# A ring of sixteen pairs of one-hot tiles in the routing stage of a layer with sixteen thousand routed rows, and another place for four products of each expert

## What is computed

```python
logits = xf @ gate_w.T
rw, sel = jax.lax.top_k(logits, TOP_K)          # TOP_K = 2
rw = jax.nn.softmax(rw.astype(jnp.float32), axis=-1).astype(x.dtype)
for e in range(E):                              # E = 8
    we = jnp.sum(jnp.where(sel == e, rw, 0.0), axis=-1)
    h = jax.nn.silu(xf @ w1[e].T) * (xf @ w3[e].T)
    out = out + h @ w2[e].T * we[:, None]
```

## Time and profile before

| what | us |
|---|---|
| median of 3 runs | 3086.04 |
| lowest and highest of them | 3084.84, 3086.20 |
| the execution that the profile shows | 3087.87 |
| its span, first to last instruction | 3086.1 |
| the routing stage in it, L1566 to L1664 | 2248.7 to 2339.6 |

### The profile page before, as it was taken

The page is one execution under the profiler, slowest core; times in us unless marked ns, Lnnn a source line. Parts: engine busy times, 40 slices in busy tenths (PEclk is TensorE's granted clock), DMA queues, the critical chain, the costliest instruction groups (busy, mean ns, idle before and its releaser), DMA issues. The chain is left out here.

```text
span 3086.1 us, 63036 instructions
## 1 busy us (share of the span) xinstructions
PE 2895.5 (94%) x22889; PEld 1807.5 (59%) x22890; DVE 2292.1 (74%) x4040; ACT 1939.0 (63%) x3559; POOL 683.5 (22%) x957
## 2 busy tenths in 40 slices
PE   5899999985999999999999999998888999999998
PEld 4777777773333333333333333337767888888886
DVE  5777777765999999999999999957775444444543
ACT  3666666660788888888888888875533333333332
POOL 2222222221000000000000000001102555555554
PEclk8998999986999999999999999998889999999999
DMA  1222332223122222222222222216642333333332
GB/s 45 97 97 96 110 110 97 101 92 104 50 82 71 85 68 66 65 71 71 72 68 69 66 67 71 72 41 211 215 138 47 50 51 48 50 49 51 49 49 41
DMA packets 170809, 243.18 MB, mean 79 GB/s; under 512 B 30952, under 2 KB 118272, under 8 KB 170576
## 3 DMA queue, kind: packets, MB, share of 16 engines
q1 hardware_dynamic: 121984, 170.70, 18.0%
q0 software_dynamic: 31152, 52.33, 8.7%
q10 hardware_dynamic: 17440, 16.98, 1.7%
HBM read 126.53 MB, written 111.21 MB: 77 GB/s over the span
## 5 line engine op out<-in xcount | busy, mean ns | idle before, releaser
L1002 DVE TENSOR_REDUCE b_mxq<-b_p_m 128x1 f32<-128x1024 f32 x1024 | 1222.1, 1222 | 70.8 <-PE b_p_m L1025 63.6
L926 ACT ACTIVATE b_probs<-b_p_e 128x512 f32<-128x512 f32 x2048 | 1105.6, 597 | 146.4 <-PE b_p_e L1073 37.8
L1025 PE MATMUL b_p_m<-b_kst,b_qst 64*128 64x512 f32 x2048 | 765.2, 454 | 26.1 <-DMA b_vst<-v_d 21.9
L1073 PE MATMUL b_p_e<-b_qst,b_kst 64*128 64x512 f32 x2048 | 747.4, 444 | 0.2 <-ACT b_probs L926 0.2
L1044 PE MATMUL b_p_o<-b_probs,b_vst 128*32 128x256 f32 x8208 | 642.1, 390 | 0.5 <-ACT b_probs L926 0.4
L1073 PEld LDWEIGHTS b_p_e<-b_qst,b_kst 64*128 64x128 f32 x2048 | 315.8, 184 | 419.3 <-ACT b_probs L926 354.9
L1812 ACT ACTIVATE d_act<-d_p_up 128x512 f32<-128x512 f32 x136 | 81.3, 598 | 491.4 <-PE d_p_up L1885 491.4
L1044 PEld LDWEIGHTS b_p_o<-b_probs,b_vst 128*32 128x32 f32 x8208 | 168.2, 108 | 324.2 <-issue 186.8
L1025 PEld LDWEIGHTS b_p_m<-b_kst,b_qst 64*128 64x128 f32 x2048 | 319.9, 188 | 57.2 <-DVE b_mxq L1002 30.9
L1781 POOL DMA_INDIRECT out_dram<-d_y,d_to x136 | 217.8, 1601 | 216.5 <-DVE d_y L1846 203.9
L1900 PE MATMUL d_p_y<-w2T,d_hT 128*128 x1096 | 259.1, 379 | 0.8 <-ACT d_hT L1806 0.8
(11 more groups left out here) (312 smaller groups left out, 4131.6 us busy)
## 6 DMA issues: line engine op xcount, KB each, us to landing
b_qst<-qk_d SPq DMA_DIRECT2D x384, 64.0 KB
b_kst<-qk_d SPq DMA_DIRECT2D x384, 64.0 KB
qk_d<-a_hi SPq DMA_DIRECT2D x32, 512.0 KB, 2.8
qk_d<-a_lo SPq DMA_DIRECT2D x32, 512.0 KB, 3.7
v_d<-a_v_s SPq DMA_DIRECT2D x16, 1024.0 KB, 4.5
b_vst<-v_d SPq DMA_DIRECT2D x64, 256.0 KB
o_d<-b_oT POOLq DMA_DIRECT2D x63, 256.0 KB, 2.7
raw<-in_L_ffn_w_dram SPq DMA_DIRECT2D x24, 512.0 KB, 4.9
```

Source lines behind the costliest of these rows:

```text
L926: nc.scalar.activation(probs[(2 * step + e % 4 // 2) % BUFS][:, (e % 2) * 512:(e % 2 + 1) * 512], p_e[(slot(e) if more1 else e) % EB][:], ...
L1002: V_.reduce_max(mxq[half][:, h, qt:qt + 1], p_m[j % 2][:], AX.X).then_inc(s["m_red"], 1)
L1025: mm(p_m[j % 2][:, kh * 512:(kh + 1) * 512], qst[r][rows(h), qt * P:(qt + 1) * P], kst[r][rows(h), kh * 512:(kh + 1) * 512], start=True, s ...
L1073: mm(p_e[u % EB][:], kst[r][rows(h), kt * P:(kt + 1) * P], qst[r][rows(h), a * 512:(a + 1) * 512], start=True, stop=True).then_inc(s["e_ps ...
```

## The change

- RING goes from 4 to 16. The pairs lie in two large tiles, `lo_tiles` and `hi_tiles`. To make room, some tiles that only the preparation uses (`iota_i`, `val_i`, `slot_i`, `of_i`, `hi_i`, `lo_i`, `first`) now share their space with ring places 8 to 15. Their instructions stay as they are.
- The four `rest` products of an expert stand between its eighth and its ninth column, no longer ahead of the first.
- `own`, `end_of` and `past` come right behind `other` on VectorE, ahead of the first pair. `p_ex` is multiplied right behind `p_rank`, in expert 0. One semaphore, `rank_ps`, is gone: `ranks` waits on `ex_ps`. `experts_of_tiles` follows `ranks`, ahead of expert 1's pairs.

```diff
+    RING = 16
+    lo_tiles, hi_tiles = sb("lo_tiles", [P, RING, P]), sb("hi_tiles", [P, RING, WIDE])
+    is_lo, is_hi = [lo_tiles[:, r] for r in range(RING)], [hi_tiles[:, r, 0:TILES] for r in range(RING)]
+    spare = [hi_tiles[:, r].bitcast(i32) for r in range(8, 14)]
...
-    RING = 4
-    is_lo = [sb(f"is_lo{r}", [P, P]) for r in range(RING)]
-    is_hi = [sb(f"is_hi{r}", [P, TILES]) for r in range(RING)]
...
         V_.tensor_scalar(other[:], chose[:], -1.0, 1.0, ALU.mult, ALU.add).then_inc(s["other_done"], 1)
+        then(V_.tensor_tensor(own[:], end[:], ident[:, 0:NE], ALU.mult))
+        then(V_.reduce_sum(end_of[:], own[:], AX.X))
+        V_.tensor_scalar(past[:], iota[:, 0:TILES], end_of[:, 0:1], None, ALU.is_ge).then_inc(s["past_done"], 1)
...
-            dve.wait_ge(s["rank_ps"], 1)
+            dve.wait_ge(s["ex_ps"], 1)
...
             if e == 1:
                 ranks()
-            if e == 2:
                 experts_of_tiles()
...
-            for b in range(4):
-                rest(e, b)
             if e == 0:
                 pe.wait_ge(s["other_done"], 1)
                 mm(p_rank, lower_r[:], other[:], start=True, stop=False, skip_group_check=True)
-                mm(p_rank[:, 1], ones_r[:], other[:, 0], start=False, stop=True, skip_group_check=True).then_inc(s["rank_ps"], 1)
-            if e == 1:
+                mm(p_rank[:, 1], ones_r[:], other[:, 0], start=False, stop=True, skip_group_check=True)
                 pe.wait_ge(s["past_done"], 1)
                 mm(p_ex, ones_b[:], past[0:NE, :], start=True, stop=True).then_inc(s["ex_ps"], 1)
...
-            for i in range(per):
+            for i in range(per // 2):
+                column(e * per + i)
+            for b in range(4):
+                rest(e, b)
+            for i in range(per // 2, per):
                 column(e * per + i)
```

More of the change, by code:

```diff
@@ L1500, in invert_places_and_transpose_weights @@
     WIDE = max(P, TILES)
-    iota_i, iota = sb("iota_i", [P, WIDE], i32), sb("iota", [P, WIDE])
+    RING = 16
+    lo_tiles, hi_tiles = sb("lo_tiles", [P, RING, P]), sb("hi_tiles", [P, RING, WIDE])
+    is_lo, is_hi = [lo_tiles[:, r] for r in range(RING)], [hi_tiles[:, r, 0:TILES] for r in range(RING)]
+    spare = [hi_tiles[:, r].bitcast(i32) for r in range(8, 14)]
+    iota_i, iota = spare[0], sb("iota", [P, WIDE])
     lanes_i, early_i, early = sb("lanes_i", [P, TILES], i32), sb("early_i", [P, 2], i32), sb("early", [P, 2])
@@ L1510, in invert_places_and_transpose_weights @@
     valid, empty_i, inv_i, choice_i, before_i = sb("valid", [P, TILES]), sb("empty_i", [P, TILES], i32), sb("inv_i", [P, TILES], i32), sb("choice_i", [P, TILES], i32), sb("before_i", [P, TILES], i32)
-    val_i, val = sb("val_i", [P, C2], i32), sb("val", [P, C2])
+    val_i, val = spare[1][:, 0:C2], sb("val", [P, C2])
     base_i, base = sb("base_i", [P, NE], i32), sb("base", [P, NE])
     total, full, full_i, tiles, end, begin = sb("total", [P, NE]), sb("full", [P, NE]), sb("full_i", [P, NE], i32), sb("tiles", [P, NE]), sb("end", [P, NE]), sb("begin", [P, NE])
-    slot_i, of_i, of, hi_i, lo_i, hi, lo = sb("slot_i", [P, C2], i32), sb("of_i", [P, C2], i32), sb("of", [P, C2]), sb("hi_i", [P, C2], i32), sb("lo_i", [P, C2], i32), sb("hi", [P, C2]), sb("lo", [P, C2])
-    first, first_sum = sb("first", [P, C2, NE]), sb("first_sum", [P, C2])
-    RING = 4
-    is_lo = [sb(f"is_lo{r}", [P, P]) for r in range(RING)]
-    is_hi = [sb(f"is_hi{r}", [P, TILES]) for r in range(RING)]
+    slot_i, of_i, hi_i, lo_i = (spare[r][:, 0:C2] for r in range(2, 6))
+    of, hi, lo = sb("of", [P, C2]), sb("hi", [P, C2]), sb("lo", [P, C2])
+    first, first_sum = lo_tiles[:, 8:16].rearrange("p r (c e) -> p (r c) e", e=NE), sb("first_sum", [P, C2])
     p_s = ctx.enter_context(nc.psum_tensor("r_p_s", [P, 512], f32))
@@ L1522, in invert_places_and_transpose_weights @@
     p_w = [ctx.enter_context(nc.psum_tensor(f"r_p_w{r}", [P, 512], f32)) for r in range(6)]
-    names = ("iotas", "other_done", "rank_ps", "past_done", "ex_ps", "pads", "pad_ps", "ones_done", "n_ps", "dve", "hot", "inv_ps", *(f"raw_in{j}" for j in range(3)), *(f"wT_ps{j}" for j in range(6)), *(f"hi_done{j}" for j in range(4)), *(f"rest_ps{j}" for j in range(4)), *(f"free{j}" for j in range(6)), "less_done")
+    names = ("iotas", "other_done", "past_done", "ex_ps", "pads", "pad_ps", "ones_done", "n_ps", "dve", "hot", "inv_ps", *(f"raw_in{j}" for j in range(3)), *(f"wT_ps{j}" for j in range(6)), *(f"hi_done{j}" for j in range(4)), *(f"rest_ps{j}" for j in range(4)), *(f"free{j}" for j in range(6)), "less_done")
     s = {n: stage_semaphore(nc, ctx, "r_" + n) for n in names}
@@ L1617, in ranks @@
             then(V_.tensor_tensor(lone[:], lone[:], begin[:], ALU.add))
-            then(V_.tensor_tensor(own[:], end[:], ident[:, 0:NE], ALU.mult))
-            then(V_.reduce_sum(end_of[:], own[:], AX.X))
-            V_.tensor_scalar(past[:], iota[:, 0:TILES], end_of[:, 0:1], None, ALU.is_ge).then_inc(s["past_done"], 1)
         def experts_of_tiles():
-            dve.wait_ge(s["ex_ps"], 1)
             then(V_.tensor_copy(ex[:], p_ex))
```

## The result

Over all runs taken beside each other the changed kernel has a median of 3074.49 us (3073.02 to 3076.98, 6 runs) against 3086.12 us (3081.99 to 3089.42, 6 runs) of the kernel before. The ratio is 0.9964, 95% interval 0.9954 to 0.9974: 0.36% faster, and clear of no change. The profiled execution took 3074.99 us, its span is 3073.2 us. In a second set of runs the ratio was 0.9967 (0.9955 to 0.9979).

The account below looks back on a forecast made before the run. VectorE and TensorE took turns, with VectorE's stops never made good; removing them gives 78.59 - 66.4 = 12.2 us, other terms nought, so 3086.04 - 12.2 = 3073.8 us, range 3071.5 to 3079.5.

Parts of the forecast that it names:

- VectorE's sum: Routing stage, first pair to behind the last: 78.59 us less 66.4 us of VectorE's work leaves 12.2 us to gain.
- The total: Whole kernel: median 3086.04 less 12.2 gives 3073.8 us, 0.40% faster.
- The clock behind the stage: Start of `experts`: TensorE's clock may rise earlier or later after the restart; put at 0 +-1.1 us.
- The low clock in expert 0: TensorE's expert 0 at 1.2 GHz after a longer idle stretch: nought, or up to 1 us if lasting into expert 1.
- the rival of a clock that stays low: TensorE in experts 0 to 7 stays at 1.2 GHz: 14.2 us an expert, 29 us more, 3115; chance 0.05.
- TensorE's own expert: Transposes, rests, pads and sixteen columns: 7.67 us an expert, under VectorE's 8.02 by 0.35.
- the rival's surcharges: TensorE becomes the bound: columns of 0.29 us, two changes at 0.27 us, 8.35 to 8.9 us an expert; chance 0.12.
- The weights: Raw matrices land in time, 1.7 us to spare: nought. Rival that they come late: gain of 7.3 us, chance 0.04.
- ScalarE: Its copies behind the rests: nought; in the last expert they end near 2323, under the columns and closing instructions.
- No effect: Rival: something other than TensorE's queue order holds VectorE at `inv_ps`, time stays at 3086; chance 0.04.

Follow-up runs that it names:

- ring4_front: The changed kernel with 4 ring places in use and the rests ahead of the first column: stage 88.26 us, ratio 0.9999 to the kernel before.
- pads_pool: The changed kernel with is_first and is_pad of all experts made by GpSimd instead of VectorE: stage 73.16 us, ratio 0.9948 to the kernel before.
- changed_again: The changed kernel run once more without edits, beside the kernel before: stage 75.61 us, ratio 0.9967.
- ring16_front: The changed kernel with all 16 ring places and the rests ahead of the first column: stage 75.72 us, ratio 0.9965 to the kernel before.
- pe_plus5: The changed kernel with five more unused TensorE products an expert behind the rests: stage 78.53 us, ratio 0.9962 to the kernel before.
- pads_pool_mid: The changed kernel with pads' one-hot tiles made by GpSimd and TensorE's pad products behind the rests: stage 71.86 us, ratio 0.9948 to the kernel before.

## Why the prediction was right

**VectorE's sum** was the whole of it: 78.59 us with stops, 66.4 us of work, 12.2 us to be had. The stretch gave 12.27. The pair stayed at 0.456 us with the new tiles, no stop was left, and the moved instructions were worth nothing (ring4_front). The closing instruction came at 2325.13 and not at the 2324.5 that I had named, because the stage began 0.7 us later, not because the stage was longer.

**The total** adds up in the profile. The spans differ by 12.9 us: the stage began 0.7 us later, the stretch gave 12.3, and the closing part 0.1. The `experts` stage gave 1.3: from its first product of `up` to the end of the span it took 737.68 us instead of 738.94. The forecast was 3073.8 us, the median 3074.49, and the medians differ by 11.6 us. That this comes so near is in part luck: single runs of the changed kernel lie 4 us apart, the late start was in no sum, and the gain in `experts` was there only as +-1.1 us for the clock.

**The clock behind the stage** was given as 0 +-1.1 us. TensorE's first product there and the granted clock around it, with expert 0's first product:

```profile
2258.27 0.38 PE L1712 MATMUL r_p_s<-r_other,lower_r 128*128 128x16 f32 x1 [3.09 <-DVE r_other L1603]
...
2335.52 0.79 PE L1887 MATMUL d_p_up<-up_hi,d_xh 128*128 x1 [1.52 <-DVE d_xl L1834]
```

```profile
2258.00:2264.00 6.00, 5.57 (x22) 5.10 (x23) 5.89 (x29) 0.20 (x1) 0.00 (x0) 0.51 0.19 70
2264.00:2265.00 1.00, 1.00 (x4) 0.81 (x3) 1.00 (x6) 1.00 (x3) 0.00 (x0) 0.52 0.00 0
...
2340.00:2341.00 1.00, 1.00 (x6) 0.82 (x5) 0.96 (x5) 0.00 (x0) 0.00 (x0) 0.97 0.00 0
```

The clock rises at about 2340.0, 4.5 us after the restart and not 6.0 as in the earlier trace rows; at about half a microsecond for each, the prediction's estimate, that is 0.7 of the 1.3 us; the rest stays open. In the eleven profiles the rise came 3.0 to 6.0 us after the restart, and the time from the restart to the end of the span was 737.3 to 738.9 us. The two don't always go together: in pads_pool the rise came after 3.2 us and the rest took 738.8, in changed_again after 4.0 and it took 737.3. So something else than this one rise moves that stage by as much, and what it is stays open.

**The low clock in expert 0** lasted longer than in the kernel before: 0.51 in 2258 to 2264, full only from about 2265.0, 6.7 us after the restart where it had been 3.4 to 4. I had allowed for it up to the end of expert 0 and given the reason why it costs nothing: 2.36 us of other work of VectorE follow. It cost nothing, and with the clock full from then to the end of the stage the rival of a clock that stays low fell; TensorE began expert 1 at 2266.64, 0.63 us behind VectorE's last pair instead of 0.36. With four places it did cost a stop of 1.07 us. That the longer idle stretch made the clock stay low longer is not shown: in ring16_front, with the rests in front, TensorE's idle stretch was 1.98 us, the shortest of all, and the clock was full only 7.1 us after the restart. The Trainium skill, TensorE: Matmul & The Clock Gate, "Why this matters for your kernels", warns that the clock falls behind idle gaps between bursts of matmuls. The trace agrees: the idle stretch of 3.09 us ended in a low clock, but so did the one of 2.08 us before.

**TensorE's own expert** was the term that was mis-sized: 7.67 us in the sum, 7.42 measured in pads_pool and 7.44 by pe_plus5. What was too dear is the column: a ready one takes 0.231 us, not 0.246, which is 0.24 us in sixteen. The eight starts that the earlier trace rows puts in one row hold a first step of 0.17 us behind the pads; the other six are 0.116 us each. Rests and pads were sized right as a sum, 1.03 + 0.08 = 1.11 us, though the parts moved: 0.81 + 0.12 for the rests and 0.17 for the pads, 1.10. The error lay on the safe side. TensorE had 0.6 us an expert to spare and not 0.35, so the rival's surcharges would have had to come to over 0.6 us to make it the bound. Its price was right in kind: pe_plus5 makes TensorE the bound and shows just this pattern.

**The weights** were not late. Landing took as long as in the earlier trace rows, with a little more at the upper end:

```profile
DMA to landing us min/median/max: 3.6/4.9/5.9
```

and no transpose waited for `raw`. **ScalarE** ended its last copies under the closing columns, as the sum had it (near 2323; 2323.75):

```profile
2321.70 2.05 ACT L1548 CAST up_lo<-r_p_w 128x512 fp32r<-128x512 f32 x4 [1.83 <-PE r_p_w L1697]
```

**No effect** is excluded: the stops went with the ring, in ring16_front with the ring alone.

## What to carry to other kernels

When two engines feed each other through a small ring and both show idle time, add up each engine's own work over one period: the larger sum is the period that a deep enough ring gives, and the ring must hold what the producer makes during the consumer's longest block of other work (here by the count a little over five pairs, a little over seven with the rests in front; 4, 6 and 16 places were run, with six falling just short). Splitting that block and deepening the ring are two cures for one stop, and their gains don't add. Count the unusual periods too: in expert 0, at the low clock, the rests in the middle stopped VectorE once with four and once with six places. Measure such a change by a stretch inside the stage that repeats to 0.1 us, and let the total only confirm it.

## What the runs showed of the hardware

- The first load of a small bf16 product that follows the rests (fp32r, 512 columns) waits 0.27 us with nothing to wait for ("issue"), so that the pads begin 1.04 us after the rests, as the row at 2287.46 of pads_pool_mid shows and the earlier trace rows too. Where an fp32 column follows the rests, in the changed kernel, it begins after 0.81 us. That looks like a saving of 0.23 us but is none: behind the fp32 column the next load comes 0.12 us late, and the pads, now behind the transposes, take 0.17 us instead of 0.08. Rests and pads together take 1.12 us in the one order and 1.10 in the other.
- GpSimd takes 2.3 to 2.5 us for the two instructions on `is_pad` of the first three experts in pads_pool and 4.2 for each later pair of them, which VectorE did in 0.6; why the later ones took longer was not tested. And VectorE's pairs beside it go from 0.456 to 0.473 us on average.
- TensorE's clock fell behind short idle stretches: 1.98 us in expert 0 of ring16_front, 2.08 in the kernel before, and 1.99 in expert 1 of pads_pool, where it had been full up to the wait and cost 1.6 us on top of it.
- The rise of TensorE's clock behind the same restart, at the start of `experts`, came between 3.0 and 6.0 us later in profiles of nearly the same code.
